# Four deformable-convolution blocks and a final one on one core: one y copy of every chunk moved to DVE, and the step's start reordered

## The chip, the cores and the metric

The kernel runs on one core of a Trainium2 chip. Times are device microseconds of one execution. The kernel before takes 4453.39 us (median of 3 runs, 4452.77 to 4454.16).

## What is computed

x is 8 images of 32 channels by 64 x 64, fp32. It is normalised per channel; then four blocks follow, each a 3x3 convolution, a convolution that gives 18 offsets per pixel, and a deformable convolution that samples at these offsets. A final deformable convolution works on two sources (the result and the normalised input, 64 channels), and x is added.

```python
def _block(x, dc_w, dc_b, of_w, of_b, dw, db):
    h = jax.nn.relu(_deconv2d(x, dc_w, dc_b))
    offset = _conv2d(h, of_w, of_b, PAD)
    return jax.nn.relu(_deform_conv2d(h, offset, dw, db))
x = _block(in_module, ...)
for i in range(1, 4):
    in_cur = x + in_prev
    x = _block(in_cur, ...)
    in_prev = in_cur
x_cat = jnp.concatenate((x, in_module), axis=1)
offset = _conv2d(x_cat, fin_off_w, fin_off_b, PAD)
return _deform_conv2d(x_cat, offset, fin_dcn_w, fin_dcn_b)
```

`_deform_conv2d` samples bilinearly: each sample is a sum over near pixels, weighted by max(0, 1-|dy|) times max(0, 1-|dx|).

## The kernel before

Images are worked on in two groups of four. A **step** is one block (layer) for one group: 8 steps for the four layers, and 2 for the final stage. Each step has a start and 32 **chunks** of 4 x 32 pixels. All five engines run their own in-order list of instructions, joined by semaphores written out by hand.

**Start of a step.** PE computes the convolution into PSUM; ACT and DVE move it to H with bias and ReLU. PE transposes H, ACT copies the transposes (L813) and SP stores them (L371) to `ht_store` in HBM. PE computes the offsets in two units of four images; DVE scales each image (L1012), takes maximum and minimum (L1015, L1016), and SP stores the result in `off_store` (L379). SP reads back offsets, spread over partitions, into HB (`load_offsets`, L389). For chunk 0, ACT takes the distance |HB + bias| (DIST, L730), DVE clamps it (L900), and POOL splits it into two fp16 halves ("hats", a cast L1076 and a subtraction L1078) in HL. The clamp of chunk 0 stands in DVE's list ahead of the fifth image. Then DVE reduces the ranges to one value (L1029 to L1035), POOL reduces over partitions (L1092), and DVE works out a flag (L1040 to L1062) that selects how the chunks are done: with one window of 11 x 11 (kind 0) or 16 x 16 (kind 1). In this profile the layers' steps run kind 0 (121 partitions) and the final ones kind 1 (128 partitions). A barrier of the five engines stands between start and chunks (`sampling`, L252 to L281).

**A chunk.** There are 12 groups g (in kind 0). For each, PE spreads the hats over window positions with 0/1 matrices (L545): `spread_y(g)` into one of 3 y slots of PSUM, then `spread_x(g)` into one of 4 x slots. ACT copies y to SBUF (YC, L761), since DVE then multiplies x from PSUM by y from SBUF into A (the "product", L895). With A, PE samples the window of pixels in VT (L563) in three parts that stand behind groups 4, 7 and 10 of the **next** chunk; ACT reads each part (L740) to SMP; the deformable sum (L576, `sums`) of the chunk before that stands behind group 1, ACT reads it (TMP, L723), and DVE adds it to X behind product 3 (L889, the "residual"). Parts and sum share one PSUM bank.

What waits for what: `spread_y(g)` for the copy of y three groups before (its slot), `spread_x(g)` for product g-4, copy g for `spread_y(g)` and product g-4, product g for copy g and `spread_x(g)`. DIST of the next chunk stands in ACT's list behind copy 1 (`next_after`, L102), its clamp in DVE's behind product 2; POOL makes the hats. SP loads offsets and windows two chunks ahead.

The places are set by a few numbers of `Shape`:

```python
self.after = {2: [4, 9], 3: [4, 7, 10], 6: [2, 4, 6, 8, 10, 11]}[count]
self.sum_after = 1
self.next_after = self.sum_after if self.batches == 1 else self.after[0]
```

## Time and profile before

| | |
|---|---|
| median of 3 runs | 4453.39 us (4452.77 to 4454.16) |
| profiled execution, its own time | 4450.75 us |
| its span | 4448.9 us |
| granted TensorE clock, mean | 0.938 |
| PE, DVE, ACT, POOL busy | 3883.5, 3017.8, 2803.3, 1140.5 us |

Busy time says how long an engine had an instruction in work, and idle time before an instruction is put down to the event that ended it. The timeline merges neighbours of one kind ("x7"), and gives in brackets the idle time before them and what ended it. The chain is followed back from the last instruction; "issue" in it is time in which nothing was waited for that the profile shows.

### The profile page before, as it was taken

To read this page: it belongs to the slowest core of one execution; us is meant where nothing else is said; L and a number is where in the kernel's file an instruction comes from. 1 tells how busy PE (TensorE), PEld (TensorE's weight loads), DVE (VectorE), ACT (ScalarE), POOL (GpSimd) and SP (SyncE) were. 2 spreads that over 40 slices of the span, in tenths; PEclk is the share of its full clock that TensorE was granted. 3 is DMA by queue.
4 is the path that set the end of the run, shared out by engine and by line. 5 is a ranking of instruction groups with operands and counts; after the bars stand their busy time and mean duration, and the time that the engine had idled before them with its cause. 6 is when DMAs were issued, how large, how long until landed. Compare 5 with 4: busy or idle time off the path is not lost.

```text
span 4448.9 us, 221697 instructions
## 1 busy us (share of the span) xinstructions
PE 3883.5 (87%) x81888; PEld 2914.2 (66%) x81888; DVE 3017.8 (68%) x5838; ACT 2803.3 (63%) x6651; POOL 1140.5 (26%) x655
## 2 busy tenths in 40 slices
PE   4998799599879969987986997798699999799998
PEld 3676576477657647765764775576577777577776
DVE  4786588388568738856874884786377776377775
ACT  2786488288558828856873884687155555255554
POOL 0332243033123303413331341332011221012211
PEclk8999899799989979998997998899799999899999
DMA  3442443244244334424433442443666664666664
GB/s 116 122 120 64 122 121 109 75 119 121 62 124 121 102 81 120 122 59 127 120 92 91 121 121 64 121 120 100 172 159 150 150 153 108 170 153 149 153 155 109
DMA packets 243252, 527.18 MB, mean 118 GB/s; under 512 B 61152, under 2 KB 151776, under 8 KB 225632
## 3 DMA queue, kind: packets, MB, share of 16 engines
q1 hardware_dynamic: 242880, 522.27, 45.2%
q8 instruction: 227, 3.72, 0.4%
q14 instruction: 145, 1.19, 0.1%
HBM read 465.57 MB, written 56.45 MB: 117 GB/s over the span
## 4 chain that ended last, share of the span: by engine, by line
PE 49%; issue 17%; DVE 14%; ACT 9%; DMA 3%; SPq 2%; DVEq 2%; ACTq 2%; POOL 1%; POOLq 1%; PEld 0%; PEldq 0%
PE P L545 19%; PE PS L563 19%; DVE A L895 11%; PE P L516 6%; ACT YC L761 5%; PE PS L576 4%; ACT DIST L730 3%; SPq L389 1%; ACT H L828 1%; POOL HL L1078 1%; DMA X<-x_dram 1%; DVEq L927 1%; PE PS L516 1%; DMA HB<-off_store 1%; DVE DIST L900 1%
## 5 line engine op out<-in xcount | busy, mean ns | idle before, releaser
L895 DVE TENSOR_TENSOR A<-P,YC 121x384 f32<-121x384 f32 (+1 forms) x4608 | 2300.1, 549 | 843.5 <-ACT YC L761 627.3
L545 PE MATMUL P<-HL,SEL 32*121 32x384 f16 (+1 forms) x21504 | 1759.7, 304 | 356.7 <-issue 202.2
L761 ACT ACTIVATE YC<-P 121x384 f32<-121x384 f32 (+1 forms) x4608 | 1719.0, 444 | 288.2 <-PE P L545 249.5
L545 PEld LDWEIGHTS P<-HL,SEL 32*121 32x121 f16 (+1 forms) x21504 | 1076.9, 116 | 807.7 <-issue 400.1
L563 PE MATMUL PS<-A,VT 121*32 121x80 f32 (+1 forms) x40960 | 1331.5, 248 | 44.1 <-ACT SMP L740 15.3
L563 PEld LDWEIGHTS PS<-A,VT 121*32 121x32 f32 (+1 forms) x40960 | 1083.3, 116 | 352.8 <-issue 176.5
L1076 POOL CAST HL<-DIST 128x1152 f16<-128x1152 f32 x320 | 366.2, 1144 | 3065.9 <-DVE DIST L900 3065.9
L740 ACT ACTIVATE SMP<-PS 128x480 f32<-128x480 f32 (+3 forms) x1152 | 593.7, 515 | 687.8 <-PE PS L563 682.6
L1078 POOL TENSOR_TENSOR HL<-DIST,HL 128x1152 f16<-128x1152 f32 x320 | 765.9, 2393 | 133.5 <-issue 74.3
L576 PE MATMUL PS<-SMP,CW 128*64 128x128 f32 x7424 | 475.9, 277 | 5.4 <-ACT SMP L740 5.4
L730 ACT ACTIVATE DIST<-HB,CONST 128x1152 f32<-128x1152 f32 x320 | 403.1, 1260 | 103.7 <-DMA HB<-off_store 101.9
L576 PEld LDWEIGHTS PS<-SMP,CW 128*64 128x64 f32 x7424 | 398.7, 137 | 86.6 <-issue 72.5
L889 DVE SCALAR_TENSOR_TENSOR X<-X,CONST,TMP 128x128 f32 (+1 forms) x320 | 280.4, 876 | 79.7 <-ACT TMP L723 79.7
L900 DVE TENSOR_SCALAR DIST<-DIST 128x1152 f32<-128x1152 f32 x320 | 240.2, 751 | 99.1 <-ACT DIST L730 99.1
L516 PE MATMUL P<-X,W 32*32 32x512 f32 x5040 | 208.9, 663 | 89.9 <-POOLq L255 58.2
L516 PEld LDWEIGHTS P<-X,W 32*32 32x32 f32 x5040 | 132.1, 107 | 139.7 <-issue 112.4
L723 ACT ACTIVATE TMP<-PS,BIAS 128x128 f32<-128x128 f32 x320 | 119.0, 372 | 150.2 <-PE PS L576 149.7
L828 ACT ACTIVATE H<-P,BIAS 32x512 f32<-32x512 f32 x128 | 87.8, 686 | 192.5 <-PE P L516 160.6
L516 PE MATMUL P<-H,W 32*32 32x512 f32 x5040 | 207.7, 636 | 1.1 <-issue 1.1
L516 PEld LDWEIGHTS P<-H,W 32*32 32x32 f32 x5040 | 137.6, 105 | 56.5 <-issue 23.1
L994 DVE TENSOR_SCALAR H<-P,BIAS 32x512 f32<-32x512 f32 x96 | 72.0, 750 | 145.2 <-PE P L516 117.8
L1012 DVE SCALAR_TENSOR_TENSOR FOFF<-P,PXB 128x512 f32<-128x512 f32 x70 | 47.8, 683 | 156.6 <-PE PS L516 99.2
(56 smaller groups left out, 667.3 us busy)
## 6 DMA issues: line engine op xcount, KB each, us to landing
HB<-off_store SPq DMA_DIRECT2D x2560, 72.0 KB, 2.4
VT<-ht_store SPq DMA_DIRECT2D x256, 512.0 KB
VT<-ht_store SPq DMA_DIRECT2D x768, 132.0 KB
VT<-ht_store SPq DMA_DIRECT2D x256, 88.0 KB
off_store<-FOFF SPq DMA_DIRECT2D x160, 128.0 KB, 2.6
ht_store<-A SPq DMA_DIRECT2D x32, 256.0 KB, 3.4
ht_store<-VT SPq DMA_DIRECT2D x32, 256.0 KB, 3.6
A<-x_dram SPq DMA_DIRECT2D x2, 2048.0 KB, 10.4
```

The costliest lines, as they stand in the source:

```text
L516: mm = nc.tensor.matmul(bank(bank0 + i)[CH * j:CH * (j + 1), :], weights[q, CH * k:CH * (k + 1)], view(row + k // 3 - 1, col + k % 3 - 1)[ ...
L545: mm = nc.tensor.matmul(dst, SEL[q, table, 0:sh.npos], hats, start=part == 0, stop=part == 1)
L563: mm = nc.tensor.matmul(PS[q:q + wide, sh.unit * v:sh.unit * (v + 1)].rearrange("p (k y x) -> p k y x", k=sh.taps, y=BLK), vt[:, img, :], ...
L576: mm = nc.tensor.matmul(PS[64 * pair:64 * (pair + 1), 0:CPX], CW[:, 64 * k:64 * (k + 1)], rhs, start=k == 0, stop=k == sh.taps - 1)
L730: nc.scalar.activation(DIST[:, :], HB[:, half, :], ACT.Abs, bias=HAT_BIAS).then_inc(abs_done, 1)
L740: nc.scalar.activation(smp_px(0, sh, b * sh.blocks + w, s, count), PS[:, 0:sh.unit * count], ACT.Copy).then_inc(ps_free, 1)
L761: nc.scalar.activation(YC[0:sh.npos, g % X_SLOTS, 0:sh.size], P[0:sh.npos, g % Y_SLOTS, 0:sh.size], ACT.Copy).then_inc(y_ready, 1)
L889: return nc.vector.scalar_tensor_tensor(dst, dst, flag, src, ALU.mult, ALU.add)
L895: return nc.vector.tensor_tensor(dst, x, y, ALU.mult)
L900: nc.vector.tensor_scalar(DIST[:, :], DIST[:, :], SCALE, SCALE, ALU.min, ALU.subtract).then_inc(clamp_done, 1)
L1076: nc.gpsimd.tensor_copy(HL[:, 0, half, :], DIST[:, :]).then_inc(hat_step, 1)
L1078: nc.gpsimd.tensor_tensor(HL[:, 1, half, :], DIST[:, :], HL[:, 0, half, :], ALU.subtract).then_inc(hats_full, 1)
```

## The change

1. `dve_copies = [6]` in kind 0 with one source: y of group 6 is copied by DVE, in front of product 6, with a semaphore of its own; `spread_y(9)`, which reuses that slot, now waits for product 6. Since `y_ready` no longer counts one per group, DVE and PE form the values of their waits by `copied`.
2. In kind 0, DIST of the next chunk stands ahead of copy 0 (`next_at = 0`), and its clamp behind product 1.
3. At a step's start the clamp of chunk 0 moves from ahead of the fifth image to behind the range reduction, and POOL makes the hats of chunk 0 behind `partition_all_reduce`.
4. ACT issues the stores to `ht_store`; SP loads the offsets of chunks 0 and 1 of a step apart.
5. H's load of x for the final stage is issued in the second step of every layer (`later_loads`), not at the final stage's start.

```diff
+        self.next_at = 0 if kind == 0 else self.after[0]
+        self.dve_copies = [6] if kind == 0 and sources == 1 else []
...
+    def copied(self, batch, g):
+        if g < 0:
+            batch, g = batch - 1, g + self.ngr
+        return batch * (self.ngr - len(self.dve_copies)) + len([k for k in range(g + 1) if k not in self.dve_copies])
...
             def layer_start(layer, final):
                 if final:
-                    load_normal(0)
...
-                    for half in range(UNITS) if final and unit == 0 else [] if final else [unit]:
-                        for n in range(BANKFULS):
-                            store_ht(sources, half, n)
...
                         load_offsets(0, 0)
-                        load_offsets(0, 1)
+                load_offsets(0, 1)
...
                     if not final and group == GROUPS - 1:
                         load_conv(layer + 1)
+                        load_normal(0)
...
+                def finish():
+                    if not final and group == GROUPS - 1:
+                        wait_alone(sp, final_loaded, 16 * (layer + 1))
...
                     def spread_y(g):
-                        pe.wait_ge(y_ready, (c * sh.batches + b) * sh.ngr + g + 1)
+                        if (g - Y_SLOTS) % sh.ngr in sh.dve_copies:
+                            pe.wait_ge(product_done, (c * sh.batches + b) * sh.ngr + g - Y_SLOTS + 1 + X_SLOTS)
+                        else:
+                            pe.wait_ge(y_ready, sh.copied(c * sh.batches + b, g - Y_SLOTS) + Y_SLOTS)
...
+                            if sh.kind == 0 and g == sh.next_at and not last:
+                                next_distance(c + 1, band + half, 1 - half)
+                            if g not in sh.dve_copies:
+                                act.wait_ge(y_full, n + 1)
...
-                            if b == 0 and g == sh.next_after and not last:
+                            if sh.kind > 0 and b == 0 and g == sh.next_at and not last:
                                 next_distance(c + 1, band + half, 1 - half)
...
+                        for n in range(BANKFULS):
+                            store_ht(unit, n)
...
-                            dve.wait_ge(y_ready, n + 1 + Y_SLOTS)
+                            if g in sh.dve_copies:
+                                wait_alone(dve, y_full, n + 1)
+                                dve.wait_ge(product_done, n + 1)
+                                nc.vector.tensor_copy(YC[0:sh.npos, g % X_SLOTS, 0:sh.size],
+                                                      P[0:sh.npos, g % Y_SLOTS, 0:sh.size]).then_inc(dve_copied, 1)
+                                dve.wait_ge(dve_copied, c + 1)
+                            else:
+                                dve.wait_ge(y_ready, sh.copied(c * sh.batches + b, g) + Y_SLOTS)
...
-                            if b == 0 and g == sh.next_after + 1 and not last:
+                            if b == 0 and g == sh.next_at + 1 and not last:
                                 clamp(c + 1)
...
-                    if n == IMG:
-                        clamp(0)
...
                 flag_count[0] += 1
+                clamp(0)
...
             def step(layer, group, bar_count, final):
-                hats(0, 0)
                 pool.wait_ge(flag_step, 4)
                 nc.gpsimd.partition_all_reduce(ST[:, 24:28], ST[:, 20:24], 128,
                                                bass.bass_isa.ReduceOp.max).then_inc(flag_step, 1)
+                hats(0, 0)
```

**DVE, in the loop over chunks, around product 6** (A is the product's output, YC the y copies). Before, products 5 and 6, each with a register instruction ahead of it:

```order
L927 REGISTER_ALU
L895 TENSOR_TENSOR A<-P,YC 121x384 [waits x_full,y_ready]
L927 REGISTER_ALU
L895 TENSOR_TENSOR A<-P,YC 121x384 [waits x_full,y_ready]
L927 REGISTER_ALU
```

Now, from product 5 to product 6:

```order
L962 REGISTER_ALU
L963 REGISTER_ALU [waits y_ready]
L922 TENSOR_TENSOR A<-P,YC 121x384 [waits x_full]
L958 COPY YC<-P 121x384 [waits y_full,product_done]
L960 REGISTER_ALU
L963 REGISTER_ALU [waits dve_copied]
L922 TENSOR_TENSOR A<-P,YC 121x384 [waits x_full]
L962 REGISTER_ALU
```

A copy stands between the two products, product 6 waits for it, and the wait for the y copies has moved from the product to a register instruction ahead of it.

**PE, in the same loop, groups 8 and 9** (each spread is two matmuls; the first of y and the first of x carry the waits). Before:

```order
L603 REGISTER_ALU
L545 MATMUL P<-HL,SEL 121x384 [waits y_ready]
L545 MATMUL P<-HL,SEL 121x384
L545 MATMUL P<-HL,SEL 121x384 [waits product_done]
L545 MATMUL P<-HL,SEL 121x384
L603 REGISTER_ALU
L545 MATMUL P<-HL,SEL 121x384 [waits y_ready]
L545 MATMUL P<-HL,SEL 121x384
L545 MATMUL P<-HL,SEL 121x384 [waits product_done]
L545 MATMUL P<-HL,SEL 121x384
```

Now:

```order
L612 REGISTER_ALU
L551 MATMUL P<-HL,SEL 121x384 [waits y_ready]
L551 MATMUL P<-HL,SEL 121x384
L617 REGISTER_ALU
L551 MATMUL P<-HL,SEL 121x384 [waits product_done]
L551 MATMUL P<-HL,SEL 121x384
L610 REGISTER_ALU
L551 MATMUL P<-HL,SEL 121x384 [waits product_done]
L551 MATMUL P<-HL,SEL 121x384
L617 REGISTER_ALU
L551 MATMUL P<-HL,SEL 121x384 [waits product_done]
L551 MATMUL P<-HL,SEL 121x384
```

`spread_y(9)` waits for a product where it waited for a copy.

**POOL, from the start of a step into its first chunks** (the plain ISA row ahead of L1092's and L1078's instruction is a load of POOL's configuration). Before:

```order
L1076 CAST HL<-DIST 128x1152 [waits clamp_done]
L1078 ISA [waits hat_step]
L1078 TENSOR_TENSOR HL<-DIST,HL 128x1152
L1092 ISA
L1092 ISA ST<-ST 128x4 [waits flag_step]
L251 ISA
L281 TENSOR_LOAD FLAG [waits bar]
L281 ISA x2
L283 COMPARE_AND_BRANCH
L1076 CAST HL<-DIST 128x1152 [waits x_full,clamp_done]
L1078 ISA [waits hat_step]
L1078 TENSOR_TENSOR HL<-DIST,HL 128x1152
```

Now:

```order
L1125 ISA
L1125 ISA ST<-ST 128x4 [waits flag_step]
L1110 CAST HL<-DIST 128x1152 [waits clamp_done]
L1112 ISA [waits hat_step]
L1112 TENSOR_TENSOR HL<-DIST,HL 128x1152
L261 ISA
L291 TENSOR_LOAD FLAG [waits bar]
L291 ISA x2
L293 COMPARE_AND_BRANCH
L1110 CAST HL<-DIST 128x1152 [waits x_full,clamp_done]
L1112 TENSOR_TENSOR HL<-DIST,HL 128x1152 [waits hat_step]
```

The load for the reduction stands ahead of everything, the one for the subtraction stands between the cast and the subtraction of chunk 0, and chunk 1 (the last two rows) has none.

## Rows read from the trace of the kernel before

**Rows 1.** The profile's page: the chain of work that ended last, by engine.
```profile
PE 49%; issue 17%; DVE 14%; ACT 9%; DMA 3%; SPq 2%; DVEq 2%; ACTq 2%; POOL 1%; POOLq 1%; PEld 0%; PEldq 0%
```

**Rows 2.** Groups of instructions by form: busy us, mean ns, idle before, releasers.
```profile
L895 DVE TENSOR_TENSOR A<-P,YC 121x384 f32<-121x384 f32 x3072 | 1531.4, 548 | 487.1 <-ACT YC L761 317.2 <-PE P L545 149.7 <-issue 19.3
...
L761 ACT ACTIVATE YC<-P 121x384 f32<-121x384 f32 x3072 | 1304.8, 499 | 207.6 <-PE P L545 207.3
...
L889 DVE SCALAR_TENSOR_TENSOR X<-X,CONST,TMP 128x128 f32 x280 | 260.7, 931 | 0.0
...
L994 DVE TENSOR_SCALAR H<-P,BIAS 32x512 f32<-32x512 f32 x96 | 72.0, 750 | 145.2 <-PE P L516 117.8 <-PE PS L516 24.8
```

**Rows 3.** Busy time by stretch, steady chunks of the first step.
```profile
130.00:390.00 260.00, 250.05 (x5691) 182.65 (x5689) 215.68 (x404) 224.01 (x494) 101.17 (x59) 1.00 0.42 117
```

**Rows 4.** Line 900, the clamp, from the fourth chunk of the first step on.
```profile
L900 DVE TENSOR_SCALAR DIST<-DIST x29: 749/750/752, 135.7 to 387.1; 128x1152 f32<-128x1152 f32 x29
```

**Rows 5.** Timeline of one steady chunk, all engines (start, us, engine, line).
```profile
207.09 0.56 DVE L895 TENSOR_TENSOR A<-P,YC 121x384 f32<-121x384 f32 x1 [0.81 <-ACT YC L761]
207.57 0.75 DVE L900 TENSOR_SCALAR DIST<-DIST 128x1152 f32<-128x1152 f32 x1
...
208.49 1.15 POOL L1076 CAST HL<-DIST 128x1152 f16<-128x1152 f32 x1 [5.30 <-DVE DIST L900]
208.70 1.08 DVE L889 SCALAR_TENSOR_TENSOR X<-X,CONST,TMP 128x128 f32 x1
...
209.70 3.33 DVE L895 TENSOR_TENSOR A<-P,YC 121x384 f32<-121x384 f32 x7
...
211.69 0.76 PE L563 MATMUL PS<-A,VT 121*32 121x80 f32 x32
...
213.38 1.31 PE L576 MATMUL PS<-SMP,CW 128*64 128x128 f32 x20
...
214.09 1.27 ACT L730 ACTIVATE DIST<-HB,CONST 128x1152 f32<-128x1152 f32 x1
...
215.48 1.28 ACT L761 ACTIVATE YC<-P 121x384 f32<-121x384 f32 x3
...
216.02 0.56 DVE L895 TENSOR_TENSOR A<-P,YC 121x384 f32<-121x384 f32 x1 [1.05 <-ACT YC L761]
```

**Rows 6.** Timeline of PE before the barrier of the first step.
```profile
82.32 1.23 PE L531 MATMUL P<-IDENT,H 128*128 128x128 f32 x8
...
105.79 2.70 PE L545 MATMUL P<-HL,SEL 32*121 32x384 f16 x16 [20.85 <-issue]
```

**Rows 7.** Timeline of DVE in the same stretch.
```profile
90.79 0.76 DVE L900 TENSOR_SCALAR DIST<-DIST 128x1152 f32<-128x1152 f32 x1 [10.16 <-ACT DIST L730]
91.47 0.68 DVE L1012 SCALAR_TENSOR_TENSOR FOFF<-P,PXB 128x512 f32<-128x512 f32 x1
...
99.69 0.16 DVE L1035 TENSOR_TENSOR ST<-ST,CONST 128x4 f32<-128x4 f32 x1
...
104.29 0.16 DVE L1062 SCALAR_TENSOR_TENSOR FLAG<-ST 128x1 int32<-128x1 f32 x1
```

**Rows 8.** Timeline of POOL in the same stretch.
```profile
93.39 2.37 POOL L1078 TENSOR_TENSOR HL<-DIST,HL 128x1152 f16<-128x1152 f32 x1 [0.52 <-POOL HL L1076]
101.79 0.39 POOL L1092 PARTITION_ALL_REDUCE ST<-ST  x1 [6.04 <-issue]
...
118.92 2.35 POOL L1078 TENSOR_TENSOR HL<-DIST,HL 128x1152 f16<-128x1152 f32 x1 [6.95 <-issue]
```

**Rows 9.** Timeline of SP's issues after that barrier.
```profile
116.66 11.97 SPq L389 DMA_DIRECT2D HB<-off_store  x24
```

**Rows 10.** Timeline of DVE in the first step of the last stage.
```profile
3115.67 2.41 DVE L1001 TENSOR_SCALAR H<-H,ST 128x4096 f32<-128x4096 f32 x1 [12.01 <-DMA H<-x_dram]
...
3165.05 0.69 DVE L1012 SCALAR_TENSOR_TENSOR FOFF<-P,PXB 128x512 f32<-128x512 f32 x1 [0.35 <-PE PS L516]
```

**Rows 11.** Waits of the last stage's first step (us, times, longest).
```profile
DVE A L895 <- DMA X<-x_dram: 9.4, 1, 9.4
```

More of the change, by code:

```diff
@@ L362, in layer_start @@
                     sp.dma_start(CW[:, 0:5 * 64], t["dcn_w"][bass.ds(layer, 1)].rearrange("a p c -> (a p) c")).then_inc(sum_loaded, 16)
-            def store_ht(sources, unit, n):
-                sp.wait_ge(ht_copied, (UNITS * (sources - 1) + unit) * BANKFULS + n + 1)
-                first, count = sheet(unit, n)
-                width = sources * 128
-                dst = bass.AP(ht_store[sources - 1].ap().tensor, (MARGIN * LANE_COLS + first) * width,
-                              [[width, count], [LANE * width, LANES], [1, width]])
-                sp.dma_start(dst, staged(sources, unit, n, count).rearrange("p (t c) -> p t c", c=width)).then_inc(ht_stored, 16)
             def store_offsets(n):
@@ L804, in step, with store_ht @@
             def step(layer, group, bar_count, final):
+                def store_ht(unit, n):
+                    sources = 2 if final else 1
+                    first, count = sheet(unit, n)
+                    width = sources * 128
+                    act.wait_ge(ht_copied, (UNITS * (sources - 1) + unit) * BANKFULS + n + 1)
+                    dst = bass.AP(ht_store[sources - 1].ap().tensor, (MARGIN * LANE_COLS + first) * width,
+                                  [[width, count], [LANE * width, LANES], [1, width]])
+                    act.dma_start(dst, staged(sources, unit, n, count).rearrange("p (t c) -> p t c", c=width)).then_inc(ht_stored, 16)
                 def keep_transposes(s, unit):
@@ L819, in step @@
                             keep_transposes(s, unit)
+                    for unit in range(UNITS):
+                        for n in range(BANKFULS):
+                            store_ht(unit, n)
                 else:
@@ L833, in step @@
                         keep_transposes(0, unit)
+                        for n in range(BANKFULS):
+                            store_ht(unit, n)
                 distance(0, 0)
@@ L998, in step @@
                 if final:
-                    dve.wait_ge(final_loaded, 16 * (group + 1))
+                    dve.wait_ge(final_loaded, 16 * (LAYERS + group))
                     nc.vector.tensor_scalar(h_view(0, 0, SIDE, SIDE), h_view(0, 0, SIDE, SIDE), norm(group, 0), norm(group, 3),
```

20 lines of the change are left out of this document (11 added, 9 removed).

## The prediction, on record before the changed kernel was run

> **What bounds the kernel now.** I read the page first. No engine holds the chain alone: PE has 49% of it, DVE 14%, ACT 9%, and 17% is issue [rows 1]. So I went by stage. The clamp shows the chunks: between chunk 3 and chunk 31 of the first step there are 29 of them from 135.7 to 387.1 us, (387.1 - 135.7) / 28 = 8.98 us each [rows 4]. With 8 steps of 30 such chunks, this loop takes about 2155 of 4449 us. In it DVE is busy 83% and ACT 86% of the time, PE 96% [rows 3], so all three have gaps, and what counts is the ring of waits. The timeline of one chunk gives it [rows 5]. DVE does product 2 at 207.09, the clamp, product 3, the residual at 208.70, products 4 to 10 without a gap from 209.70, 0.476 us apart (3.33 / 7). Product 6, the third of these, ends at 209.70 + 0.95 + 0.55 = 211.20. Only then may PE do `spread_x(10)`, and part 2 of the samples behind it starts at 211.69; then come group 11 and groups 0 and 1 of the next chunk, the sum at 213.38 to 214.69, `spread_y(2)`, copy 2 at 215.48 and product 2 at 216.02. The ring is 8.93 us long, and product 6's place on DVE is one of its links.
>
> Three more things are to be seen. The residual takes 931 ns on average in 280 cases [rows 2]; in this chunk it takes 1.08 us and ends at 209.78, just after POOL's cast ended (208.49 + 1.15 = 209.64) [rows 5]. Before the fifth image of a step DVE waits 10.16 us for DIST of chunk 0 [rows 7]. And POOL waits 6.04 us before the reduction and 6.95 us before the subtraction of chunk 1 [rows 8], with a load of its configuration ahead of each in POOL's order, while the subtraction of chunk 0, whose code was there, waited 0.52.
>
> **Part by part.** Sums are made against the profiled execution's own 4450.75 us; the median of 4453.39 is 2.6 us above it, and I do not scale for that.
>
> *The copy on DVE.* It reads 384 columns from PSUM. The nearest rows are the product of the same size (548 ns, 0.476 apart in a run) and a PSUM-sourced tensor_scalar of 512 columns (750 ns) [rows 2, 5]; per column above a fixed part both are at one rate, so 0.55 us until its end is seen, 0.47 of occupancy. Product 6 waits for that end, and a register instruction lies between wait and product: 0.12 us, an estimate from the 0.03 to 0.1 us between other waits and starts. So product 6 comes 0.67 us later. Bounds: 0.4 (copy as quick as ACT's spacing of 0.42, 1.26 / 3, no extra wait) and 0.8. ACT is relieved of 0.4 us, worth nothing unless ACT is in the ring there; it isn't between copies 6 and 10, which run ahead of the products.
>
> *`spread_y(9)` waits for product 6.* Before, PE had done `spread_y(9)` and `spread_y(10)` while product 6 ran, and only `spread_x(10)` was left: 211.20 to 211.69 is 0.49 us to part 2. Now y9, x9, y10 and x10 all stand behind product 6. y and x of one group go through the same rows of the array, so x9 comes some 0.37 us after y9: 0.9 us to part 2, 0.4 us more. Bounds 0.2 and 0.5.
>
> *DIST first, clamp behind product 1.* DIST (1.27 us, 1.15 of ACT's time) goes ahead of copies 0 and 1 instead of behind. Products 0 and 1 come later, and DVE's idle 1.05 us before product 2 [rows 5] moves ahead of product 0. The ring now runs over DVE's product 0, with the clamp inside it as before, and no longer over the sum and the TMP read. There is a gain: cast and residual overlap less. The cast starts 0.92 us after the clamp starts (207.57 to 208.49) and ends at +2.07; the residual, now behind products 2 and 3, can start at +1.60 instead of +1.13, and ends at +2.2 either way. One product is done in time that the residual had spent blocked: 0.47 us.
>
> The Trainium skill (SBUF — State Buffer, the section on the doors to SBUF) says that VectorE and GpSimd share an exclusive port pair, and that a VectorE instruction with two SBUF inputs waits out a GpSimd instruction that reads SBUF; the residual's end 0.14 us behind the cast's agrees with it.
>
> *The new ring, added up from product 0.* Product 1 at 0.47, clamp 0.94, products 2 and 3 at 1.60 and 2.07, residual 2.54 to 3.15 (the cast's end plus 0.15), product 4 at 3.07, 5 at 3.54, the copy at 4.01, product 6 at 4.68, done at 5.23. Part 2 at 6.15, done 6.91 (0.76); ACT's read of it 0.34 and copy 11 (0.37), with 0.08 of starts: 7.70; DIST to 8.85; copy 0 done 9.35 (0.50); product 0 at 9.48. That is 0.50 above 8.98. The same kind of sum for the kernel before comes out at 8.82 where 8.98 was measured, so I take between 0.50 and 0.66: **0.6 us per chunk, 8 x 30 x 0.6 = +144 us.**
>
> *Start of a layer's step.* The conv of unit 1 ends at 82.32 [rows 6], so image 5 starts at 82.4 instead of 91.47, and the ranges are done at 99.85 - 9.1 = 90.8 [rows 7]. POOL's reduction, its load long done, follows at once (before, it came 1.9 us behind the ranges). But now POOL does the cast of chunk 0 from 91.8 to 92.9, then the load of some 6 to 7.5 us [rows 8], then the subtraction, 2.4 us: all this ahead of the barrier, which POOL reaches at 101.2 to 102.8. Before, the last engine came at 104.45 and PE started 1.34 us later [rows 6, 7]; now 102.5 to 104.1 against 105.79. **2.5 us per step, -20 us.** The subtraction of chunk 1, which ended at 121.3 and held PE, comes 7 us sooner, but that is not gained: ACT now does DIST of chunk 2 ahead of copy 0 of chunk 1, and needs offsets of which SP issued the last some 3.7 us after 116.66 [rows 9], landing near 123. Before, that DIST came two copies later. I put +1.5 us per step for chunks 0 and 1 with their own DVE copies: **+12 us** (bounds -20 and +30).
>
> *ht_store from ACT, offsets of chunk 1 later.* ACT issues five stores while PE's second unit or DIST is awaited; nothing waits for ACT there. Cover gone, it would be 3 to 4 us a step.
>
> *The final stage.* DVE waited 12.01 us for H [rows 10]; x is there already, but PE has X's transposes to do first, so about 8 us are saved, once: **-8 us**. Its fifth image waited only 0.35 us, for PE [rows 10]: nothing to gain there, while cast, load and subtraction go ahead of its barrier: about 6.5 us later in each of 2 steps, **+13 us**. Chunk 1's earlier hats are worth nothing there, since DVE waits for X to land (9.4 us) [rows 11]. *The four loads of x* (2 MB each) go behind the first loads in the second step of each layer and ahead of the windows of chunk 2: 0 to 5 us each, **+8 us**.
>
> Sum: 144 - 20 + 12 - 8 + 13 + 8 = +149: 4450.75 + 149 = **4600 us**.
>
> **The rivals.** *The copy is covered* (chance 0.15). DVE is idle 17% of a chunk, 1.5 us, and 0.67 fits in; then the shorter wait of the residual and ACT's relief are all that is left, -0.1 to -0.4 us per chunk: 4450.75 + 5 - 60 = 4396 us. For it speaks the idle time; against, that this idle time lies ahead of products 11, 0 and 2, not before product 6. It decides if part 2 starts no later than before, seen from the clamp. *It balances* (0.06): the ring grows by less than 0.04 us, about 4450 us.
>
> *The copy itself is blocked by POOL* (0.06). It would start near +3.07 us from the clamp; POOL's subtraction runs from +2.25 to +4.65. If DVE's copy had to wait for it, 1.5 us more per chunk: 4600 + 360 = 4960 us. Against it: 512 columns from PSUM take as long as the clamp's 1152 from SBUF (750 ns both) [rows 2, 4], so the PSUM read isn't in the quick form that the clamp has; and products run through the subtraction undisturbed.
>
> *PE's clock.* Its granted clock is 1.00, the 2.4 GHz level, in the steady chunks [rows 3]. More idle PE could lower it; I include that above 4690 us, chance 0.05.
>
> **How the numbers follow.** Forecast 0.68; covered 0.15; balanced 0.06; blocked 0.06; clock 0.05. The forecast's own bounds are 0.3 to 0.9 us per chunk, 4530 to 4675 us. For 8 in 10 the range leaves out blocked, clock and most of covered: 4440 to 4690. A change of 0.2% (9 us) is what a measurement can tell. Faster 0.15, same 0.06, slower 0.79.
>
> **What would show it.** Right: clamps 9.5 to 9.7 us apart; product 6 0.67 us behind the start of DVE's copy; `spread_y(9)` released by DVE's product; part 2 0.9 us behind product 6's end; residual near 0.6 us; idle DVE ahead of product 0; POOL's long wait between cast and subtraction ahead of the barrier and none in chunk 1; the last stage's barrier 6 us later. Wrong: chunks of 8.98 us or less, a copy of 2 us, or a granted clock under 1.00 in the loop.

## The result, and the profile after

| | before | changed |
|---|---|---|
| median of 4 runs | 4453.08 us | 4805.97 us (4795.80 to 4832.44) |
| ratio | | 1.0803, 95% interval 1.0754 to 1.0851 |
| profiled execution, its own time | 4450.75 us | 4796.69 us |
| its span | 4448.9 us | 4794.8 us |
| granted TensorE clock, mean | 0.938 | 0.908 |

The change makes the kernel slower by 353 us. The forecast said slower, by 147 us, and its range ended at 4690. I went by stage again, with the clamp as the mark of a chunk. From chunk 3 to chunk 31 of the first step the clamps now stand so (count, duration, first and last start):

```profile
L927 DVE TENSOR_SCALAR DIST<-DIST x29: 748/749/751, 136.3 to 428.2; 128x1152 f32<-128x1152 f32 x29
```

That is (428.2 - 136.3) / 28 = 10.43 us a chunk, where before it was 8.98 [rows 4]. Over the eight steps of the layers, these stretches of 28 chunks took 2327.1 us, against 2015.5 before: 312 of the 346 us between the two spans. The starts of steps and chunks 0 to 2 make up 17 us in the layers and 17 in the final stage, where the chunks themselves kept their 17.5 to 17.9 us (all these are of one execution each). So the loop of the layers is where to look, and there two things happened.

**First, the ring of waits grew.** The timeline of one undisturbed chunk of the changed kernel (start, duration, engine, line; in brackets the idle time before and what ended it), as in [rows 5]:

```profile
184.24 1.02 DVE L922 TENSOR_TENSOR A<-P,YC 121x384 f32<-121x384 f32 x2 [0.97 <-ACT YC L773]
...
185.18 0.75 DVE L927 TENSOR_SCALAR DIST<-DIST 128x1152 f32<-128x1152 f32 x1
...
186.09 1.14 POOL L1110 CAST HL<-DIST 128x1152 f16<-128x1152 f32 x1 [5.95 <-DVE DIST L927]
...
186.77 0.61 DVE L916 SCALAR_TENSOR_TENSOR X<-X,CONST,TMP 128x128 f32 x1
...
187.30 1.01 DVE L922 TENSOR_TENSOR A<-P,YC 121x384 f32<-121x384 f32 x2
...
188.24 0.54 DVE L958 COPY YC<-P 121x384 f32<-121x384 f32 x1
...
188.90 1.49 DVE L922 TENSOR_TENSOR A<-P,YC 121x384 f32<-121x384 f32 x3
...
189.51 1.05 PE L551 MATMUL P<-HL,SEL 32*121 32x384 f16 x8 [0.31 <-DVE A L922]
...
190.50 0.76 PE L569 MATMUL PS<-A,VT 121*32 121x80 f32 x32
...
192.37 0.56 DVE L922 TENSOR_TENSOR A<-P,YC 121x384 f32<-121x384 f32 x1 [0.65 <-ACT YC L773]
192.38 1.25 ACT L739 ACTIVATE DIST<-HB,CONST 128x1152 f32<-128x1152 f32 x1
...
192.71 1.31 PE L582 MATMUL PS<-SMP,CW 128*64 128x128 f32 x20
...
194.15 1.02 DVE L922 TENSOR_TENSOR A<-P,YC 121x384 f32<-121x384 f32 x2 [1.23 <-PE PS L582]
...
195.09 0.75 DVE L927 TENSOR_SCALAR DIST<-DIST 128x1152 f32<-128x1152 f32 x1
```

The clamps at 185.18 and 195.09 are 9.91 us apart; undisturbed chunks take 9.67 and 9.92 us in turn. DVE's copy starts at 188.24 and product 6 at 188.90, 0.66 later. It ends about 0.55 later, at 189.45; `spread_y(9)`, the x8 row of PE, is released by it at 189.51 with an idle PE before, and part 2 starts at 190.50, 1.05 us behind product 6's end, where it was 0.49. The residual takes 0.61 us and follows the cast. DIST stands ahead of copy 0, and DVE's longest idle time is now before product 0, 1.23 us. By form (busy, mean ns, idle before):

```profile
L922 DVE TENSOR_TENSOR A<-P,YC 121x384 f32<-121x384 f32 x3072 | 1569.6, 550 | 789.6 <-ACT YC L773 445.6 <-PE P L551 265.5 <-PE PS L582 45.7
...
L916 DVE SCALAR_TENSOR_TENSOR X<-X,CONST,TMP 128x128 f32 x280 | 196.3, 701 | 0.0
L958 DVE COPY YC<-P 121x384 f32<-121x384 f32 x256 | 138.7, 542 | 0.0
```

The residual's mean went from 931 to 701 ns [rows 2]; it would be lower but for the slow chunks below, since every undisturbed chunk has 0.61 us. The copy takes 542 ns, the 0.55 us that I took from the product. DVE's idle time ahead of products went up from 487.1 to 789.6 us: DVE works more and waits more, as a ring that runs over several engines makes it.

**Second, TensorE's granted clock fell inside the loop**, which it did not before. The windows view of the same 28 chunks, and of one stretch in them (length; busy time and instructions of PE, PEld, DVE, ACT, POOL; then PEclk, DMA share, GB/s):

```profile
136.30:429.00 292.70, 279.32 (x5522) 204.91 (x5524) 221.52 (x423) 212.85 (x450) 99.09 (x56) 0.93 0.38 102
211.70:218.50 6.80, 6.80 (x89) 4.90 (x86) 3.72 (x7) 3.87 (x8) 2.73 (x2) 0.51 0.43 126
```

The mean is 0.93 where it was 1.00 [rows 3], and from 211.7 to 218.5 it is 0.51: the 1.2 GHz level. What such a stretch costs is in PE's own rows around it:

```profile
209.09 1.05 PE L551 MATMUL P<-HL,SEL 32*121 32x384 f16 x8 [0.32 <-DVE A L922]
210.08 0.76 PE L569 MATMUL PS<-A,VT 121*32 121x80 f32 x32
210.77 2.21 PE L551 MATMUL P<-HL,SEL 32*121 32x384 f16 x12
212.91 2.40 PE L582 MATMUL PS<-SMP,CW 128*64 128x128 f32 x20
...
216.73 1.83 PE L569 MATMUL PS<-A,VT 121*32 121x80 f32 x48
...
216.92 2.39 POOL L1112 TENSOR_TENSOR HL<-DIST,HL 128x1152 f16<-128x1152 f32 x1 [0.18 <-POOL HL L1110]
...
218.06 1.39 DVE L916 SCALAR_TENSOR_TENSOR X<-X,CONST,TMP 128x128 f32 x1
...
219.30 1.04 PE L569 MATMUL PS<-A,VT 121*32 121x80 f32 x48
...
221.58 1.05 PE L551 MATMUL P<-HL,SEL 32*121 32x384 f16 x8 [0.45 <-DVE A L922]
```

Ahead of it PE did what it does in each chunk, with an idle 0.32 us before y9. Then the sum of 20 matmuls takes 2.40 us instead of 1.31, and the part of 48 takes 1.83 instead of 1.04. From this y9 to the next it is 12.49 us (209.09 to 221.58).

Not all of that is PE's own time. Products 2 and 3 wait for PE, so the residual behind them starts 3.38 us after its clamp (214.68 to 218.06) instead of 1.60. By then POOL has passed from its cast to its subtraction, and the residual takes 1.39 us instead of 0.61: it ends at 219.45, 0.14 us behind the subtraction (216.92 + 2.39). These two, 1.78 and 0.78 us, are the 2.57 us by which this chunk is longer than an undisturbed one (12.23 against 9.66). In the eight steps 43 of the 224 chunks between chunk 3 and chunk 31 are lengthened like this, by 1.5 to 4.3 us, 131 us together, and in 40 of the 43 the residual takes 1.3 to 2.6 us. Its extra time adds up to some 40 us: the slow clock costs partly by pushing a DVE instruction into POOL's longer one.

The page's row of the clock in 40 slices hardly shows the slow stretches, since a slice is 120 us long and every start of a step lowers one anyway. Of the changed kernel, with its chain, and of the kernel before:

```profile
PEclk8999799879978998997999899799989999899999
...
PE 52%; DVE 14%; issue 14%; ACT 7%; SPq 5%; DMA 3%; POOLq 2%; ACTq 1%; DVEq 1%; POOL 0%; PEld 0%; PEldq 0%
```

```profile
PEclk8999899799989979998997998899799999899999
```

The mean of the whole run tells more (0.908 against 0.938), and the windows view of a stretch without starts most. In the chain, the part of ACT went from 9% to 7% and that of PE from 49% to 52% [rows 1]: nothing in it points at the DVE copy, which has 2%. The chain tells where the last waits ended; why PE was slow isn't in it.

### The profile page after: what moved, and what is told of

Its sections match the earlier page's. It is cut to its first block, busy times and chain, and to the rows that moved or that the text cites. A ratio compares the mean times of both kernels' runs of the same rounds, so it can differ in the third digit from the quotient of the medians.

```text
span 4794.8 us, 224163 instructions
## 1 busy us (share of the span) xinstructions
PE 4188.9 (87%) x81888; PEld 3140.9 (66%) x81888; DVE 3120.8 (65%) x6094; ACT 2759.9 (58%) x6395; POOL 1140.4 (24%) x655
## 4 chain that ended last, share of the span: by engine, by line
PE 52%; DVE 14%; issue 14%; ACT 7%; SPq 5%; DMA 3%; POOLq 2%; ACTq 1%; DVEq 1%; POOL 0%; PEld 0%; PEldq 0%
PE P L551 20%; PE PS L569 18%; DVE A L922 9%; PE PS L582 6%; PE P L522 6%; ACT YC L773 5%; SPq L389 3%; DVE YC L958 2%; DVE X L916 2%; POOLq L265 2%; SPq L397 2%; PE PS L522 1%; DMA HB<-off_store 1%; ACT H L853 1%; DMA X<-x_dram 1%
## 5 line engine op out<-in xcount | busy, mean ns | idle before, releaser
L922 DVE TENSOR_TENSOR A<-P,YC 121x384 f32<-121x384 f32 (+1 forms) x4608 | 2338.5, 550 | 1166.7 <-ACT YC L773 780.3
L551 PE MATMUL P<-HL,SEL 32*121 32x384 f16 (+1 forms) x21504 | 1995.2, 311 | 413.2 <-issue 223.7
L773 ACT ACTIVATE YC<-P 121x384 f32<-121x384 f32 (+1 forms) x4352 | 1673.8, 437 | 326.0 <-PE P L551 278.5
L551 PEld LDWEIGHTS P<-HL,SEL 32*121 32x121 f16 (+1 forms) x21504 | 1241.2, 119 | 920.4 <-issue 369.1
L569 PE MATMUL PS<-A,VT 121*32 121x80 f32 (+1 forms) x40960 | 1359.3, 253 | 33.2 <-ACT SMP L749 15.3
L569 PEld LDWEIGHTS PS<-A,VT 121*32 121x32 f32 (+1 forms) x40960 | 1108.0, 119 | 341.5 <-issue 245.8
L582 PE MATMUL PS<-SMP,CW 128*64 128x128 f32 x7424 | 532.2, 298 | 5.4 <-ACT SMP L749 5.4
L582 PEld LDWEIGHTS PS<-SMP,CW 128*64 128x64 f32 x7424 | 447.0, 149 | 100.5 <-issue 86.4
L916 DVE SCALAR_TENSOR_TENSOR X<-X,CONST,TMP 128x128 f32 (+1 forms) x320 | 212.4, 664 | 79.7 <-ACT TMP L732 79.7
L927 DVE TENSOR_SCALAR DIST<-DIST 128x1152 f32<-128x1152 f32 x320 | 239.8, 749 | 12.1 <-ACT DIST L739 12.0
```

What stands on the lines that cost most here:

```text
L551: mm = nc.tensor.matmul(dst, SEL[q, table, 0:sh.npos], hats, start=part == 0, stop=part == 1)
L569: mm = nc.tensor.matmul(PS[q:q + wide, sh.unit * v:sh.unit * (v + 1)].rearrange("p (k y x) -> p k y x", k=sh.taps, y=BLK), vt[:, img, :], ...
L582: mm = nc.tensor.matmul(PS[64 * pair:64 * (pair + 1), 0:CPX], CW[:, 64 * k:64 * (k + 1)], rhs, start=k == 0, stop=k == sh.taps - 1)
L773: nc.scalar.activation(YC[0:sh.npos, g % X_SLOTS, 0:sh.size], P[0:sh.npos, g % Y_SLOTS, 0:sh.size], ACT.Copy).then_inc(y_ready, 1)
L916: return nc.vector.scalar_tensor_tensor(dst, dst, flag, src, ALU.mult, ALU.add)
L922: return nc.vector.tensor_tensor(dst, x, y, ALU.mult)
```

## The experiments

All times are medians of all runs of a kernel. Runs of one group stood beside their own runs of the kernel before, whose medians were 4450.6 to 4451.7 us.

| kernel | us | ratio to before (95%) |
|---|---|---|
| no_dve_copy | 4392.32 | 0.9872 (0.9855 to 0.9888) |
| start_only | 4484.10 | 1.0076 (1.0059 to 1.0093) |
| copy_dist_late | 5157.15 | 1.1582 (1.1562 to 1.1601) |
| y9_after_copy | 4545.97 | 1.0204 (1.0184 to 1.0224) |
| change_filled | 4670.22 | 1.0492 (1.0474 to 1.0509) |
| copy_late_filled | 4960.46 | 1.1147 (1.1128 to 1.1165) |
| copy_11 | 4377.18 | 0.9835 (0.9816 to 0.9854) |
| copy_8 | 4652.56 | 1.0452 (1.0429 to 1.0475) |
| copy_8_y11_early | 4404.15 | 0.9895 (0.9879 to 0.9912) |
| before_dist_first | 4369.55 | 0.9813 (0.9800 to 0.9826) |
| before_copy_11 | 4366.56 | 0.9810 (0.9796 to 0.9823) |
| start_old_clamp | 4475.40 | 1.0048 (1.0032 to 1.0063) |
| start_old_x | 4481.00 | 1.0057 (1.0041 to 1.0072) |
| start_stores_offsets | 4470.96 | 1.0048 (1.0032 to 1.0065) |
| start_stores | 4471.03 | 1.0044 (1.0027 to 1.0061) |

### The DVE copy against the rest of the change

**no_dve_copy:** the change without its copy on DVE.

```diff
-        self.dve_copies = [6] if kind == 0 and sources == 1 else []
+        self.dve_copies = []
```

> All of the change but the DVE copy: ACT copies the y of group 6 again, y9 waits for that copy. Theory A (the copy on DVE lengthens the ring and, by PE's longer waits, brings the granted clock down in the loop): no stretch at the 1.2 GHz level inside the chunks of a layer's step, clamps about 8.4 us apart by the same hand-made sum of the ring (8.98 before), so about 4453 - 0.5 x 240 = 4330 us, 4300 to 4400. Rival B (DIST ahead of copy 0 is what costs, the copy is hidden): clamps over 9.3 us apart, half-clock stretches still there, over 4650 us. Rival C (the new start of a step costs): steady chunks as in A, but over 4450 us.

Measured: 4392.32 us. The 28 chunks of the first step, in the windows view:

```profile
137.30:377.40 240.10, 240.10 (x5490) 183.42 (x5488) 197.51 (x394) 214.50 (x477) 99.70 (x56) 1.00 0.42 124
```

240.10 / 28 = 8.58 us a chunk, PE busy all the time, clock 1.00. All but the copy is a gain of 58 us; the copy with what hangs on it costs 4805.97 - 4392.32 = 414 us. Theory A stands, though the hand-made sum of 8.4 was 0.18 short. In the second step of a layer, where the early loads of x run, the clock of this kernel is 0.98 to 1.00.

**start_only:** also without DIST first. `next_at` is 1 in kind 0, and DIST stands behind that copy.

```diff
-        self.next_at = 0 if kind == 0 else self.after[0]
+        self.next_at = 1 if kind == 0 else self.after[0]
...
-                            if sh.kind == 0 and g == sh.next_at and not last:
-                                next_distance(c + 1, band + half, 1 - half)
...
-                            if sh.kind > 0 and b == 0 and g == sh.next_at and not last:
+                            if b == 0 and g == sh.next_at and not last:
```

> Only the changes outside the loop (clamp of chunk 0 behind the range reduction, hats of chunk 0 behind the reduction over partitions, stores of H's transposes from ACT, x loaded earlier); in the chunks DIST behind copy 1, the clamp behind product 2 and all copies on ACT, as before. By the recorded terms: -20 (start) -8 (x for the final stage) +13 (final barrier) +8 (loads of x), and without the +12 of chunks 0 and 1 or with it: 4440 to 4460 us, clamps 8.98 us apart, no half clock in the loop. Rival C (the start costs a good part of the +353 us): over 4500 us.

Measured: 4484.10 us, outside what I expected: changes 3 to 5, with the rewritten waits of change 1 that this kernel keeps, cost 33 us. Not all of it lies outside the loop: the stretches of 28 chunks take 2033.8 us here, 18 more than in the kernel before. DIST first gives back 4484.10 - 4392.32 = 92 us.

**copy_dist_late:** the same edit as start_only, but the copy of group 6 stays on DVE.

> As the change, but DIST behind copy 1 and the clamp behind product 2, as before: the DVE copy on the old order. Theory A: the copy's 0.66 us and the later part 2 lie on the ring in full, since the ring still runs over the sum and product 2: clamps 9.9 to 10.1 us apart where the clock is full, half-clock stretches at least as often as in the change, 4800 to 4950 us. Rival B (DIST first is what costs): clamps near 9.0 to 9.3 and under 4600 us.

Measured: 5157.15 us, worse than expected. Undisturbed chunks are 10.22 and 10.48 us long in turn, a little over the 9.9 to 10.1 of the sum, but most are not undisturbed; over 28 chunks it is 11.74 us each, at a mean clock of 0.82:

```profile
136.90:465.60 328.70, 301.18 (x5491) 215.11 (x5487) 228.60 (x421) 217.70 (x449) 98.62 (x56) 0.82 0.31 91
```

PE's rows show up to two idle gaps in a chunk, before y9 and before x4 (the row of 2 matmuls), both until a product ended:

```profile
190.06 1.05 PE L551 MATMUL P<-HL,SEL 32*121 32x384 f16 x8 [0.78 <-DVE A L920]
...
198.28 0.53 PE L551 MATMUL P<-HL,SEL 32*121 32x384 f16 x2 [0.28 <-DVE A L920]
```

So DIST first was no cost here; it made the copy cheaper, mostly by the clock: in undisturbed chunks the copy adds 1.31 us here (10.35 against the 9.04 of start_only) and 1.21 in the change (9.79 against 8.58). And the clock loses more where PE is kept waiting more.

**y9_after_copy:** one wait of the change is made shorter.

```diff
-                            pe.wait_ge(product_done, (c * sh.batches + b) * sh.ngr + g - Y_SLOTS + 1 + X_SLOTS)
+                            pe.wait_ge(dve_copied, c + 1)
```

> As the change, but spread_y(9) waits for the DVE copy of y 6 itself (its slot is free then), not for product 6. If the wait for product 6 is what puts part 2 at +0.9 instead of +0.49 us: 0.2 to 0.5 us less per chunk, clamps 9.3 to 9.6 us apart at full clock, and PE waits less before part 2, so fewer half-clock stretches: 4580 to 4720 us. Rival D (only DVE's own occupancy counts, PE's wait for product 6 is covered by the wait of spread_x(10) for the same product): 4790 to 4830 us, as the change.

Measured: 4545.97 us, better than expected: 260 us of the 414 hang on this one wait.

```profile
136.70:396.10 259.40, 259.40 (x5490) 195.53 (x5488) 210.48 (x422) 209.41 (x449) 99.20 (x56) 1.00 0.40 115
```

```profile
186.69 2.42 DVE L922 TENSOR_TENSOR A<-P,YC 121x384 f32<-121x384 f32 x5
...
187.77 0.76 PE L569 MATMUL PS<-A,VT 121*32 121x80 f32 x32
```

The chunk is 259.40 / 28 = 9.26 us, against 8.58 without the copy: 0.69 us for the copy's own place on DVE. Part 2 starts 187.77 - (186.69 + 0.55) = 0.53 us behind product 6's end, near the 0.49 of before. PE has no gap, and the clock is 1.00 in all 28 chunks (0.99 to 1.00 in the other steps of the layers).

### The clock

**change_filled:** the change, with x of group 8 spread three times over in the time in which PE would wait. Nothing is left out, and nobody waits for a new event.

```diff
-                            mm = spread(sh, g, b, half, table, Y_SLOTS + g % X_SLOTS, sh.size * tile)
+                            for again in range(3 if sh.kind == 0 and g == 8 else 1):
+                                mm = spread(sh, g, b, half, table, Y_SLOTS + g % X_SLOTS, sh.size * tile)
```

> As the change, but in kind 0 PE does spread_x(8) three times over before it signals, 4 more matmuls of 384 columns a chunk, in the time in which it would wait for product 6; nothing else changes, and the result is the same. Theory A1 (the half-clock stretches inside the loop come from PE's idle time ahead of y9; keep it busy and they go): no or few stretches at 1.2 GHz in the loop, clamps 9.8 us apart on average, up to 10.0 if product 8 then waits for its x; 4640 to 4720 us instead of 4806. Rival E (the stretches have another cause, such as the DVE copy, DMA load or chance): half clock in the loop as often as in the change, and 4800 to 4860 us.

Measured: 4670.22 us, 136 us less than the change, with 4 matmuls a chunk more.

```profile
134.50:408.70 274.20, 274.20 (x5601) 210.08 (x5600) 214.69 (x421) 210.23 (x449) 99.12 (x56) 1.00 0.37 109
```

```profile
196.51 2.25 PE L551 MATMUL P<-HL,SEL 32*121 32x384 f16 x16
198.68 0.76 PE L569 MATMUL PS<-A,VT 121*32 121x80 f32 x32
```

The gap is gone (16 matmuls in one run up to part 2), the clock is 1.00 in all 28 chunks, and the chunk is 274.20 / 28 = 9.79 us, the mean of the undisturbed 9.67 and 9.92. So these two things are apart: the longer ring is 0.81 us a chunk against the kernel before, and the slow stretches are another 136 us. The residual is back at 0.61 us in these chunks, so its share went with them. Theory A1 holds, and rival E falls, since DVE's copy is as it was.

**copy_late_filled:** the same filling on copy_dist_late.

> The same filling (spread_x(8) three times) on the kernel with the DVE copy and DIST behind copy 1, in which nearly every chunk had a stretch at 1.2 GHz. Theory A1: clamps near its undisturbed 10.2 us, most half clock gone, 5157 - (11.96 - 10.3) x 240 = 4760 us, 4700 to 4900. Rival E: 5100 to 5250 us.

Measured: 4960.46 us; 197 us of the expected 400 came back. Its mean clock over 28 chunks of the first step is 0.92 instead of 0.82. I had filled one of two gaps; PE still waited 8.8 us for products in these chunks (27.0 before the filling), and stretches at 1.2 GHz remained.

**copy_8 and copy_8_y11_early:** the change with `dve_copies = [8]`, and the same with `spread_y(11)` waiting for DVE's copy (the edit of y9_after_copy, which now acts on y11).

> As the change, but DVE copies the y of group 8 (spread_y(11) waits for product 8). By the hand-made sum the copy is then behind product 6 and so not ahead of part 2, but ahead of products 8 to 11: clamps about 8.9 us apart at full clock. Theory F: 4440 to 4540 us, with little or no half clock in the loop. Rival G: clamps 9.2 to 9.8, over 4560 us.

Measured: 4652.56 us, with 4601.85 to 4718.49 the widest spread of all (4644.83 without the highest run). The expectation of 4440 to 4540 us failed. Undisturbed chunks are 8.92 and 9.18 us long, as summed, but the clock again falls:

```profile
134.80:403.60 268.80, 257.09 (x5492) 190.05 (x5488) 217.30 (x422) 213.16 (x450) 99.42 (x56) 0.94 0.38 111
```

```profile
303.12 0.76 PE L569 MATMUL PS<-A,VT 121*32 121x80 f32 x32
304.27 1.94 PE L551 MATMUL P<-HL,SEL 32*121 32x384 f16 x12 [0.39 <-DVE A L922]
```

The gap is now behind part 2, before y11, 0.39 us.

> copy_8, but spread_y(11) waits for the DVE copy of y 8, not for product 8. In copy_8 PE has one gap of 0.39 us in a chunk, ahead of y11, and half-clock stretches in the loop; in the change one of 0.31 us ahead of y9, and stretches; in y9_after_copy none, and no stretches. Theory A1 (the gap brings the clock down): the gap goes, and so do the stretches in the loop; clamps 8.8 to 9.1 us apart; 4480 to 4550 us instead of 4653. Rival E (the stretches come with a DVE copy at 8, or by chance): still half clock in the loop, 4600 us or more.

Measured: 4404.15 us, better than expected by 76 us.

```profile
135.40:375.80 240.40, 240.40 (x5489) 179.62 (x5488) 207.98 (x421) 210.60 (x448) 99.65 (x56) 1.00 0.42 124
```

No gap, clock 1.00, and 240.40 / 28 = 8.59 us: the copy at group 8 costs nothing that can be seen in the chunk. The median is 12 us above no_dve_copy's; the profiled executions have this at the steps' starts, not in the loop. Since the same copy stands at the same place, it was the wait that cost, once by the ring (9.05 to 8.59, 0.46 us a chunk) and once by the clock.

### The place of the copy

> As the change, but DVE copies the y of group 11 instead of 6 (spread_y(2) of the next chunk then waits for product 11). Theory F (what a DVE copy costs is its place: ahead of product 6 it stands on the ring to part 2, ahead of product 11 DVE is idle anyway, and ACT had to read part 2 before copy 11): clamps 8.0 to 8.5 us apart, no half clock in the loop, 4280 to 4400 us, faster than the kernel before. Rival G (any 0.66 us on DVE costs 0.66 us a chunk): clamps about 9.2 and 4540 us or more.

**copy_11** is the change with `dve_copies = [11]`; `spread_y(2)` of the next chunk then waits for product 11. It measured 4377.18 us: the same operation, at another place, is 429 us cheaper than at group 6. Undisturbed chunks are 7.98 and 8.3 us long. From the second half of the step on every other one is longer, since PE then waits for something else, the windows from HBM:

```profile
276.73 1.04 PE L569 MATMUL PS<-A,VT 121*32 121x80 f32 x48 [1.18 <-DMA VT<-ht_store]
```

So the ring can be shortened to 8.0 us, but the loads don't follow.

### The start of a step

> start_only, but the clamp of chunk 0 ahead of the fifth image and the hats of chunk 0 ahead of the reduction over partitions again; the stores from ACT and the early loads of x stay. If the order of clamp and hats costs what start_only lost in the final stage (12 us there, 0 to 3 us elsewhere): 4484 - 12 = 4472 us, down to 4460. Rival (in the layers' steps the new order gains 2.5 us each, as its first step shows): 4484 - 12 + 18 = 4490 us.

**start_old_clamp** puts clamp and hats of chunk 0 back (the diff of change 3, reversed, on start_only). Measured: 4475.40 us, 9 us less. From the last clamp of a step to the clamp of the next one's chunk 3, the two final steps take 325.1 instead of 339.6 us, and the layers' steps together some 8 us more (1071.5 against 1063.7).

> start_only, but x for the final stage is loaded at the final stage's start again, not in every layer. Steady chunks of the steps of the second group were 1.6 to 5.3 us longer with a clock stretch at 1.2 GHz in most, 8 us in all, and the saved wait at the final stage was up to 8 us. If these are the same thing: 4484 us within 5. If the loads of x cost more than they save: 4470 to 4480 us. If the wait saved counts for more: 4485 to 4492.

**start_old_x** puts the load of x for the final stage back (change 5). Measured: 4481.00 us, 3 us less, which the interval can't tell from none. But inside it are two amounts: the 28 chunks of the four second steps are 12.1 us shorter together, and the first final step's start is 8.1 us longer, since DVE again waits 12.2 us for H there.

> The kernel before with only this of the change: the stores of H's transposes issued by ACT instead of SP, and the offsets of chunk 1 loaded behind those of the second unit. My recorded price was 0. Start_only lost 33 us; 9 of them went with the old clamp order and 3 with the old loads of x. If the stores and offsets are the rest: 4470 to 4476 us. Rival (the parts act on each other): 4451 to 4460 us.

**start_stores_offsets** is start_only with both put back, so that only change 4 and the rewritten waits are left. Measured: 4470.96 us. With start_only, start_old_clamp and start_old_x it makes a square, in which each of the two parts can be read twice. The loads of x cost 12.1 and 12.3 us in the chunks and save 8.1 and 10.7 at the first final start. The new order of clamp and hats costs 14.5 and 12.8 us in the final steps; in the starts of the layers' steps it is 7.8 us shorter in one pair and 5.9 us longer in the other, so these starts differ from execution to execution by as much as was to be read.

> As start_stores_offsets, but the offsets of chunks 0 and 1 are loaded together behind the first unit, as before; only the stores are issued by ACT. If ACT's issue of the stores, ahead of the distance of chunk 0, costs: 4465 to 4476 us. If the later offsets of chunk 1 cost: 4451 to 4458 us.

**start_stores** also loads the offsets of chunks 0 and 1 together again. Measured: 4471.03 us. So the later offsets cost nothing, and 20 us (interval 12 to 27) go to what is left: the stores issued by ACT, and the rewritten waits, which put a register instruction more ahead of PE's spreads and DVE's products. No pair of runs takes these two apart. ACT's rows at the first step's start, in start_stores:

```profile
84.86 3.25 ACTq L822 DMA_DIRECT2D ht_store<-VT  x4
88.73 1.25 ACT L738 ACTIVATE DIST<-HB,CONST 128x1152 f32<-128x1152 f32 x1 [3.69 <-DMA HB<-off_store]
```

ACT issues stores (x4 here, behind one at 84.39) and then does DIST, which waits for its offsets to land anyway. In this first step nothing is lost. Over the layers' steps the starts add up to about 8 us more, the first final step has 5, and the 28 chunks of each layer's step are longer by 0.2 to 1.4 us, 6 us in all. No store to `ht_store` is issued in those chunks. From the start of part 2 to the sum, where PE only has spreads to do, it is 1.84 us on average before and 1.86 in before_dist_first, but 1.95 in start_stores and 2.01 in copy_11 and in before_copy_11; the last has the rewritten waits and SP's stores. So those 6 us are the waits' and not ACT's. By which wait the other 14 come was not found; it stays open.

### The best version

> The kernel before with one change alone: in kind 0 DIST ahead of copy 0 and the clamp behind product 1; start of a step, final stage and copies as before. Theory: the order inside the chunk is worth 8.98 - 8.585 = 0.4 us a chunk (no_dve_copy against start_only: -93 us), and the new start of the steps costs 33 us by itself, so without it 4451 - 95 = 4355 us, 4345 to 4370. Rival H (both act on each other, the new start is part of the gain): 4380 to 4410 us.

**before_dist_first** is the kernel before with change 2 alone. Measured: 4369.55 us, at the upper end of what I expected.

> The kernel before with DIST first and the y of group 11 copied by DVE, start of a step and final stage as before. If the parts add up: 4377 - 33 = 4344 us, 4330 to 4360, faster than every kernel so far; the gain over DIST first alone only 10 to 20 us, since chunks of 8.0 us now and then wait for the load of their windows. Rival: where the loads bound it, nothing is left, 4355 to 4380 us.

**before_copy_11** adds DVE's copy at group 11. Measured: 4366.56 us, above the 4330 to 4360 of the sum and inside the rival's range, 1.9% faster than the kernel before and 9.1% faster than the change. The two differ by 3 us, within their spread (4362.96 to 4374.44 and 4358.58 to 4372.72). Chunks in both are 8.5 to 8.6 us on average; with the copy the gain in the ring is taken back by waits for the loads. The simple one, without a copy on DVE, is as good.

## Why the prediction was right and where it failed

By differences of medians the 353 us are made up so, within 2 us: 33 for changes 3 to 5 and the rewritten waits, -92 for DIST first, +154 for the copy on DVE (y9_after_copy against no_dve_copy), +124 for `spread_y(9)` behind product 6 (change_filled against y9_after_copy), +136 for the clock, with the residuals that it delays.

**The bound.** Right: the ring of waits bounds a chunk, and product 6 is one of its links. The copies at 8 and 11 show the other side of it: at 11, and at 8 with y11 waiting for the copy, they cost nothing.

**The copy, 0.67 us.** Right: 0.66 in the timeline, 0.69 in the ring. That the idle 17% of DVE doesn't cover it was right as well.

**`spread_y(9)` behind product 6, part 2 at 0.9 us.** Right in mechanism; the size was 1.05 us, so 0.53 more in the ring instead of 0.4. PE starts y9 within 0.06 us, as I took it, but its four spreads take 0.99 us until part 2 (189.51 to 190.50), more than I had put them at. In change_filled against y9_after_copy the wait is worth 9.79 - 9.26 = 0.53 us a chunk.

**DIST first.** Right in sign and size: 8.98 to 8.58, 0.40 us where one product's 0.47 was named, and the residual went from 1.08 us to 0.61 in no_dve_copy's and before_dist_first's chunks. What I did not see is that the same blocking returns, by POOL's subtraction, wherever PE is slow and the residual comes late. The Trainium skill (SBUF — State Buffer, SBUF: two separate sides) was weighed there, and the trace agrees: the residual ends at 187.38, again 0.15 us behind the cast's end (186.09 + 1.14).

**The sum for a chunk.** 0.6 us, with 0.50 to 0.66 to choose from, and 0.81 measured: -0.40 + 0.69 + 0.53. I took a value between the sum and its correction, where the upper one, plus the missing 0.13 of y9, was right. In the chunk shown above, product 0 comes 9.91 us after the one before (184.24 to 194.15) where the sum had 9.48: part 2 starts 0.11 us later than in the sum, and from its end to DIST it is 1.12 us (191.26 to 192.38) where 0.79 was put for ACT's read and copy 11. The term was short by 0.21 x 240 = 50 us.

**PE's clock, "above 4690 us, chance 0.05".** This is the step that failed. The mechanism was named, but it had no term in the sum and no price, and I counted it as unlikely because the row of before said 1.00 in the loop. The runs showed 0.93 there, in stretches of 1.2 GHz, and it costs 136 us, of which some 40 are residuals held by POOL's subtraction. The forecast of 4600 with 50 more for the ring and 28 more for what lies outside it (33 for my 5) is 4678; change_filled measured 4670, and the rest is the clock. The prediction had itself put `spread_y(9)` and all behind it after product 6, with PE idle until then, and the chunk longer for the same work of PE; that should have raised the chance of this rival. The trace before shows both levels at the steps' starts, so that the cost of slow matmuls could have been read. How often the clock would fall could not, and nor could the delayed residual without following the ring through a slow chunk: most of the lengthened chunks have 2.57 us more, or 4.0 to 4.2.

**The start of a layer's step, -2.5 us, and chunks 0 and 1, +1.5.** In the rows of the changed kernel the fifth image starts at 82.49, the clamp stands behind the ranges, and DVE then waits for chunk 1:

```profile
82.49 0.69 DVE L1045 SCALAR_TENSOR_TENSOR FOFF<-P,PXB 128x512 f32<-128x512 f32 x1 [1.73 <-PE P L522]
...
91.34 0.76 DVE L927 TENSOR_SCALAR DIST<-DIST 128x1152 f32<-128x1152 f32 x1 [0.47 <-ACT DIST L739]
...
124.16 1.02 DVE L922 TENSOR_TENSOR A<-P,YC 121x384 f32<-121x384 f32 x2 [9.85 <-ACT YC L773]
```

```profile
91.01 0.39 POOL L1125 PARTITION_ALL_REDUCE ST<-ST  x1 [85.96 <-DVE ST L1068]
92.28 1.14 POOL L1110 CAST HL<-DIST 128x1152 f16<-128x1152 f32 x1 [0.88 <-DVE DIST L927]
101.14 2.35 POOL L1112 TENSOR_TENSOR HL<-DIST,HL 128x1152 f16<-128x1152 f32 x1 [7.72 <-issue]
...
109.69 2.37 POOL L1112 TENSOR_TENSOR HL<-DIST,HL 128x1152 f16<-128x1152 f32 x1 [0.18 <-POOL HL L1110]
```

```profile
104.86 5.85 PE L551 MATMUL P<-HL,SEL 32*121 32x384 f16 x36 [19.86 <-issue]
```

```profile
122.50 1.25 ACT L739 ACTIVATE DIST<-HB,CONST 128x1152 f32<-128x1152 f32 x1 [8.86 <-DMA HB<-off_store]
```

POOL's reduction follows the ranges at 91.01; the wait for the load of the configuration (7.72 us) is ahead of the barrier, and chunk 1's subtraction has none, as said. PE starts at 104.86 instead of 105.79 [rows 6], 0.9 us sooner and not 2.5, since the subtraction ended at 103.49, behind the 102.8 that I had as its latest. ACT's DIST of chunk 2 waits 8.86 us for offsets and holds the copies of chunk 1 behind it, as said: that gives back what the barrier gained. The forecast for both terms together was -8 us. In start_only against start_old_clamp the eight starts are 7.8 us shorter, in start_old_x against start_stores_offsets 5.9 us longer, so the agreement of the first pair is luck, and these starts alone don't show the size. The medians of the two pairs are 9 and 10 us apart; with the final stage's 14.5 and 12.8 us taken off, 3 to 6 us are left as the gain of the order in the eight steps.

**The final stage.** Its barrier was forecast at +13; by start_old_clamp it is 339.6 - 325.1 = 14.5 us, and 12.8 in the other pair. H's load was forecast at -8; it is -8.1 and -10.7. The four loads of x were forecast at +8 and cost 12.1 and 12.3, all of it in chunk 3 or 4 of each of these steps, which waits 1.1 to 5.2 us longer; a stretch at 1.2 GHz stands at that place in three of the four.

**ht_store from ACT, "nothing waits for ACT there".** Wrong as far as it can be told: 20 us, not 0, for this and the rewritten waits, which had no term either and have 6 of the 20. I costed both at nothing by looking at one step's start. The price that I named for a lost cover, 3 to 4 us a step, was also too high.

## What to carry to other kernels

Where an operation is moved to an engine with idle time, its price is set by what stands behind it on that engine: the same copy costs 414 us ahead of product 6 and nothing ahead of product 11. Release a buffer by the event that frees it, not by a later one of the same engine: one such wait was 260 us, over half of them with TensorE's clock. When a change makes TensorE wait a little in every turn of a loop, price a fall to 1.2 GHz beside the wait itself, and test it by giving TensorE harmless work in the gap. Then follow what the slow stretch delays: here a DVE instruction came so late that it met POOL's 2.39 us subtraction instead of the end of its cast.

## What I had not expected of the hardware

More matmuls made the kernel faster: 4 more per chunk, 136 us less, since the granted clock stayed at 2.4 GHz. The stretches at 1.2 GHz came where PE waited 0.31 to 0.39 us for a product once a chunk (the change, copy_8), and more often with gaps of 0.28 and 0.78 us (copy_dist_late). They don't follow from the length of a gap alone: the kernel before had one of 0.25 to 0.27 us in its chunks and no stretch, and copy_11 waited up to 1.2 us for a load, in 12 of its 28 chunks, and also kept its clock in the first step. In before_copy_11 the longest wait of that step, 1.65 us until 263.85, was followed by a stretch at 1.2 GHz from 264.1 us on. The Trainium skill (TensorE: Matmul & The Clock Gate, the second failure mode, by PSUM queue cycling) says that short idle moments of TensorE between groups of matmuls can make its clock go back and forth; the trace agrees, with the clock of 0.51 between 211.7 and 218.5 us. What exactly a gap must be like was not found here.
